# Attention of a tuned transformer kernel: maxima turned late, a longer lead of the query-major scores, rests in PSUM, value products in runs of two blocks

## The reference, cut to what matters

```python
# attention A: 16 query heads of 16, one shared key head and value head, causal
scores = einsum('bnhd,bmd->bhnm', q, k) / sqrt(16);  scores = where(causal, -inf, scores)
out = einsum('bhnm,bmd->bnhd', softmax(scores), v)
# attention B: 16 heads with their own keys and values, causal, with an ALiBi bias
scores = einsum('bhqd,bhkd->bhqk', q, k) / sqrt(16) + slope[h] * (kpos - qpos)
```

## Time and profile before

| | |
|---|---|
| median of the runs | 1035.86 us |
| profiled execution: its time, its span | 1033.63 us, 1031.9 us |
| TensorE busy (matmuls) | 964.2 us, 93% |
| VectorE busy | 760.6 us, 74% over the kernel |
| ScalarE, GpSimd busy | 570.4 us, 411.3 us |
| first attention, first piece to last value product | 55.0 to 296.7 us |
| second attention, the same | 571.9 to 806.5 us |
| a step inside an attention | 27.8 us |

### The profile page before, as it was taken

One profiled execution on the slowest core, in us unless ns is written; L12 is line 12 of the kernel. 1 busy time (PEld: TensorE's weight loads), 2 busy tenths in 40 slices (PEclk: granted clock), 3 DMA queues, 4 the chain that ended last, 5 costly groups with the idle time before them and its releaser, 6 DMA issues.

```text
span 1031.9 us, 19370 instructions
## 1 busy us (share of the span) xinstructions
PE 964.2 (93%) x6370; PEld 613.2 (59%) x6370; DVE 760.6 (74%) x2132; ACT 570.4 (55%) x1078; POOL 411.3 (40%) x434
## 2 busy tenths in 40 slices
PE   4888999999889999999998989999999899999998
PEld 3433333333358889988886433333334588899887
DVE  6798999999256776447778979999992568764475
ACT  4525777777744335653354647777777533466332
POOL 3420634333435417625843102323225361374570
PEclk9879999999989999999999989999999999999999
DMA  4721212210105215733249523334401251266351
GB/s 142 193 46 30 47 44 44 44 44 9 49 26 203 80 47 173 181 122 120 67 116 218 118 36 69 61 70 77 76 13 44 84 173 53 82 190 160 117 183 48
DMA packets 66755, 95.40 MB, mean 92 GB/s; under 512 B 19669, under 2 KB 50821, under 8 KB 64599
## 3 DMA queue, kind: packets, MB, share of 16 engines
q1 hardware_dynamic: 46645, 52.74, 19.0%
q10 hardware_dynamic: 13100, 22.53, 8.6%
q0 software_dynamic: 6912, 18.88, 7.0%
HBM read 66.79 MB, written 26.67 MB: 91 GB/s over the span
## 4 chain that ended last, share of the span: by engine, by line
PE 71%; DVE 16%; issue 4%; DMA 3%; ACT 3%; POOL 2%; SPq 1%; ACTq 0%; DVEq 0%; POOLq 0%
PE o_ps L1101 13%; PE st_ps L1084 8%; PE su_ps L1043 7%; PE st_ps L293 7%; PE st_ps L294 7%; PE st_ps L295 7%; PE o_ps L1241 4%; PE st_ps L1043 4%; PE su_ps L1241 3%; DVE mab L1729 3%; PE su_ps L1147 3%; DVE unread L1725 3%; PE st_ps L1276 2%; DVE xn L1604 1%; PE su_ps L293 1%
## 5 line engine op out<-in xcount | busy, mean ns | idle before, releaser
L1446 ACT ACTIVATE pt<-st_ps 128x512 f32<-128x512 f32 (+1 forms) x584 | 312.0, 596 | 161.3 <-PE st_ps L1084 153.5
L1084 PE MATMUL st_ps<-qs,ks 99*128 99x512 bf16 (+9 forms) x768 | 211.8, 328 | 4.3 <-DMA qs<-nmx 2.4
L807 POOL TENSOR_SCALAR_AFFINE_SELECT pt<-pt 128x512 f32<-128x512 f32 x120 | 74.7, 641 | 311.7 <-ACT pt L1446 311.7
L1043 PE MATMUL su_ps<-ks,qs 102*128 102x512 bf16 (+7 forms) x538 | 155.2, 330 | 11.5 <-DVE mc L1725 4.5
L1101 PE MATMUL o_ps<-pt,vp 128*32 128x512 f32 (+3 forms) x1536 | 156.6, 505 | 0.0
L1725 DVE CUSTOM_DVE_ANT_0 unread<-su_ps,cst 128x384 f32<-128x384 f32 (+3 forms) x324 | 143.0, 479 | 16.2 <-PE su_ps L1043 15.5
L1729 DVE TENSOR_REDUCE mab<-su_ps 128x1 f32<-128x512 f32 (+2 forms) x181 | 118.6, 683 | 7.2 <-PE su_ps L1043 5.1
L1043 PEld LDWEIGHTS su_ps<-ks,qs 96*128 96x128 bf16 (+1 forms) x538 | 48.5, 98 | 122.4 <-DVE mab L1729 44.4
L888 POOL DMA_INDIRECT rows_in<-rows,source x80 | 79.1, 989 | 97.5 <-DVE source L1988 73.7
L1084 PEld LDWEIGHTS st_ps<-qs,ks 99*128 99x128 bf16 (+2 forms) x768 | 73.1, 98 | 63.5 <-ACT pt L1446 16.6
L1472 ACT CAST hh<-hf 128x512 fp32r<-128x512 f32 x64 | 39.7, 620 | 123.2 <-DVE hf L1943 123.2
(11 more groups left out here) (234 smaller groups left out, 1975.7 us busy)
## 6 DMA issues: line engine op xcount, KB each, us to landing
wu_raw<-w_units_dram SPq DMA_DIRECT2D x32, 384.0 KB, 3.2
outs<-rows_out ACTq DMA_DIRECT2D x40, 256.0 KB
q_parts<-hml SPq DMA_DIRECT2D x16, 384.0 KB, 3.1
wexp_raw<-w_units_dram SPq DMA_DIRECT2D x16, 384.0 KB, 6.5
inv<-inverses SPq DMA_DIRECT2D x128, 32.0 KB, 1.8
rows<-xn SPq DMA_DIRECT2D x8, 512.0 KB, 6.2
qs<-q_parts ACTq DMA_DIRECT2D x10, 384.0 KB
k_parts<-hml SPq DMA_DIRECT2D x8, 384.0 KB, 2.9
```

The lines of the kernel that those rows point to most:

```text
L807: pool.affine_select(block, block, [[0, 4], [1, P]], ALU.is_ge, 0.0, base=0, channel_multiplier=-1).then_inc(masked, 1)
L1043: last = pe.matmul(out_b[:, c0:c0 + width], query_columns(s, slice(0, rows), j0 + a, P * qt, P * qt + P), key_stack(l, s)(j0 + a)[0:rows, ...
L1084: last = pe.matmul(out_b[:, at:at + hi - lo], key_stack(l, s)(j)[0:rows, P * kt:P * kt + P], query_columns(s, slice(0, rows), j, lo, hi), ...
L1446: act.activation(exponentials(S, q)[:, j, 0:width_of(s, q)], bank[KM_BANKS[i % len(KM_BANKS)]][:, 0:width_of(s, q)], ACT.Exp, scale=1 / np ...
```

## The change

1. The value products are issued in runs: `(0,), (1, 2), (3, 4), (5, 6), (7, 8)` of each later step, each behind the second piece of the block two after the last of the run. In step 0 they are `(0,)`, `(1, 2)`, `(3, 4)`, `(5, 6)` and `(7, 8, 9)`, the last one ahead of the first piece of step 1. The run `(7, 8)` of a step stands in the next step's block 1, as block 8 did.
2. `lead` is 0.36 where it was 0.2.
3. For steps 2 to 6 of each attention (`turned_late`) the transposition stands behind the third unit of the following step; unit numbers, and with them the banks, are counted accordingly. VectorE does the join at once and the negative parts three units later. SyncE sends these maxima ahead of `gather_sums(S, 0)`.
4. The rest of the maxima is written back to the PSUM bank of the transposition (`turned[:, P:2 * P]`) where it went to the SBUF tile `nmr`. The bank is given free by the last of the four operations, where the second gave it free.
5. The reciprocals stand ahead of units 10 and 26, where they stood ahead of 6 and 27.

```diff
+def value_runs():
+    first = len(FIRST_BLOCKS)
+    runs = {2: (0,), 6: (3, 4), 8: (5, 6)}
+    early = {HALF_BLOCKS: (1, 2), first: (7, 8, 9)}
+    for s in range(1, STEPS):
+        for run in ((0,), (1, 2), (3, 4), (5, 6), (7, 8)):
+            runs[block_base(s) + run[-1] + PV_LAG] = tuple(block_base(s) + q for q in run)
+    return runs, early, runs.pop(block_base(STEPS) + PV_LAG - 1)
+
+def turned_late(s):
+    return 2 <= s < STEPS - 1
+
+def unit_number(S, u):
+    s = S % STEPS
+    if u == NSU - 1 and turned_late(s):
+        return unit_base(S) + u + UNITS_AHEAD
+    if u < UNITS_AHEAD and turned_late(s - 1):
+        return unit_base(S) + u - 1
+    return unit_base(S) + u
+UNITS_AHEAD = 3
...
     for s in range(2, STEPS):
-        for u, t in enumerate(s - 1 - lead + through):
+        for u in range(NSU):
+            t = s - 1 - lead + (passed[u] if turned_late(s - 1) else through[u])
             while at[n] < t - 1e-9 or u > 1 and n < FIRST_PIECES - 1:
                 n += 1
-            behind[n].append((s, u))
+            if u < NSU - 1 or not turned_late(s):
+                behind[n].append((s, u))
+            if u == UNITS_AHEAD - 1 and turned_late(s - 1):
+                behind[n].append((s - 1, NSU - 1))
...
-UNITS_BEHIND = [units_behind_pieces(l, 0.2) for l in range(2)]
+UNITS_BEHIND = [units_behind_pieces(l, 0.36) for l in range(2)]
-INVERT_AT, DIVIDE_BEHIND = (6, 27), (2, 4)
+INVERT_AT, DIVIDE_BEHIND = (10, 26), (2, 4)
...
-                    if n in (HALF_PIECES, FIRST_PIECES):
-                        for early in range(i - PV_LAG, i):
-                            values(l, 0, early)
+                    if j == 0:
+                        for b in EARLY_RUNS.get(i, ()):
+                            values(l, *place_of_block(b))
                     key_major(l, s, q, j)
-                    if j == PV_BEHIND and i >= PV_LAG and i not in [...]:
-                        values(l, *place_of_block(i - PV_LAG))
+                    if j == PV_BEHIND:
+                        for b in RUNS.get(i, ()):
+                            values(l, *place_of_block(b))
...
-            def negative_parts(src, rows, a, taken, count, done):
+            def negative_parts(turned, rows, a, taken, count, done):
+                src, rest = turned[:, 0:P], turned[:, P:2 * P]
                 dve.tensor_scalar(nmx[rows, a, 0, :], src, -1.0, None, ALU.mult).then_inc(nm_step, 1)
-                dve.scalar_tensor_tensor(nmr[rows, :], src, -1.0, nmx[rows, a, 0, :], ALU.mult, ALU.subtract).then_inc(taken, 1)
+                dve.scalar_tensor_tensor(rest, src, -1.0, nmx[rows, a, 0, :], ALU.mult, ALU.subtract).then_inc(nm_step, 1)
-                dve.tensor_copy(nmx[rows, a, 1, :], nmr[rows, :]).then_inc(nm_step, 1)
+                dve.tensor_copy(nmx[rows, a, 1, :], rest).then_inc(nm_step, 1)
-                dve.tensor_tensor(nmx[rows, a, 2, :], nmr[rows, :], nmx[rows, a, 1, :], ALU.subtract).then_inc(nm_done, 1)
+                dve.tensor_tensor(nmx[rows, a, 2, :], rest, nmx[rows, a, 1, :], ALU.subtract).then_inc(taken, 1)
...
+                            if u == UNITS_AHEAD and turned_late(s):
+                                maxima_parts(l, s)
                             maximum(l, s + 1, u)
-                        maxima_parts(l, s + 1)
+                        join_maxima(l, s + 1)
+                        if not turned_late(s + 1):
+                            maxima_parts(l, s + 1)
```

More of the change, by code:

```diff
@@ L161, in place_of_block, with run_behind, taking @@
     return next((s, i - block_base(s)) for s in reversed(range(STEPS)) if i >= block_base(s))
+def value_runs():
[6 more added lines that the diff above has]
+    return runs, early, runs.pop(block_base(STEPS) + PV_LAG - 1)
+PV_LAG = 2
+RUNS, EARLY_RUNS, LAST_RUN = value_runs()
+def run_behind(b):
+    return next((i for i, run in RUNS.items() if b in run), None)
+def taking(b):
+    i = run_behind(b)
+    if i is None:
+        i = next((i for i, run in EARLY_RUNS.items() if b in run), None)
+    return None if i is None else 4 * i + 3
 def unit_base(S):
     return NSU * S - len(range(0, S, STEPS))
+def turned_late(s):
[8 more added lines that the diff above has]
+UNITS_AHEAD = 3
 ADDED = [[u for u in range(len(SU)) if SU[u][5] and not by_matmul(s, u)] for s in range(STEPS)]
@@ L186, in added_before @@
     at = added_turn(S, u) - 2
-    return unit_base(added_units(S)[at][0]) + added_units(S)[at][1] + 1 if at >= 0 else 0
+    return unit_number(*added_units(S)[at]) + 1 if at >= 0 else 0
 def units_behind_pieces(l, lead):
@@ L452, in program @@
         half_in, first_in, turned_half, half_taken = [sem("half_in0"), sem("half_in1")], sem("first_in"), sem("turned_half"), sem("half_taken")
[L453 removed]
+        su_ready, su_used, mc_done, nm_step = (sem(n) for n in ("su_ready", "su_used", "mc_done", "nm_step"))
         st_ready, p_ready, pv_done, ou_done, inv_done, ot_done = (
@@ L635, in send_half @@
             def send_half(l, half):
-                sp.wait_ge(nm_done, maxima_count(l, 0, half))
+                sp.wait_ge(half_taken, 2 * l + half + 1)
                 for part in range(3):
@@ L710, in attention @@
                         load_unit(l, 0)
-                    if s + 1 < STEPS:
+                    if s + 1 < STEPS and not turned_late(s + 1):
                         send_maxima(l, s + 1)
@@ L1132, in attention @@
                         output_projection(l, FC_BEHIND[4 * q + j])
-                for q in range(len(LATER_BLOCKS) - PV_LAG, len(LATER_BLOCKS)):
-                    values(l, STEPS - 1, q)
+                for b in LAST_RUN:
+                    values(l, *place_of_block(b))
             def output_projection(l, tt):
@@ L1449, in attention @@
                             load_stack(l, s + 2, LOAD_BEHIND.index(n))
-                        if s and n == 4 * PV_LAG - 1:
+                        own = piece_base(s) + n
+                        if s and own == taking(block_base(s - 1) + last_of(s - 1, 1)[0]):
                             take_output(S - 1, 1)
-                        if n == 4 * (last_of(s, 0)[0] + PV_LAG + 1) - 1:
+                        if own == taking(block_base(s) + last_of(s, 0)[0]):
                             take_output(S, 0)
```

35 lines of the change are left out of this document (19 added, 16 removed).

## The result

The changed kernel takes 1063.42 us (median of 4 runs, 1061.68 to 1068.51), the kernel before, beside it on the same chip, 1035.35 us: ratio 1.028, interval [1.024, 1.032]. It is slower, and 1059 was predicted. The profiled execution has a span of 1061.8 us.

What follows compares the result with a forecast made beforehand. TensorE and VectorE, both near their limit and tied by three banks, were taken as the bound. Terms 11.4 + 10.4 + 1.6 = +23.4 us on 1033.6 gave 1057.0, plus 2.2 for the median: 1059, range 1036 to 1067 (likeliest case 1053 to 1067).

Steps and rivals of the forecast that it cites:

- The rule for a stretch: Between value products: 2.09 us (2.95 with a run of two) plus VectorE's first N-3 units, or TensorE's time if that decides.
- VectorE's account: In a later step VectorE has 24.7 us of work and 4.5 dry, giving the same as the walked 29.2 us.
- the first rival: TensorE is the bound and the mergings count: 26 us faster, 1010 us; chance 0.11.
- At least 1.1 us dry per run of two: Behind each run of two VectorE idles at least 1.1 us; under 0.5 us would show the forecast wrong.
- Waits of TensorE's units for L1725 and L1729 of some 3 us per step: Sign in a later step: TensorE's units wait some 3 us in all for VectorE at these lines.
- Steps 0 and 1: Start of both attentions: longer lead and runs end step 0 5.6 us later, step 1 takes 0.4 less; +10.4 us.
- The second rival: Front-loaded units are paid back in full and the long run sees full clock: 1049 to 1053 us; chance 0.27.
- steps 6 and 7: End of both attentions: step 6 net +1.5 us, step 7 -0.7 us in each; +1.6 us for both.
- The fourth rival: TensorE's longer waits bring the clock down inside most steps, over +14 us: above 1067 us; chance 0.08.
- three mergings: In step 7, without units, output projections keep ScalarE ahead, so three mergings give their full 0.24 us each: -0.7 us.
- 1 to 2 us a step: Price if the reciprocal ahead of unit 10, some 5 us behind the copy of the sums, is uncovered.
- +0.3 a turned step from L1740: In 10 turned steps L1740, the last operation on the maxima, falls from 0.60 to 0.28 us, saving 0.3 us each.

Runs made afterwards that it cites:

- VectorE relieved: Changed kernel and kernel before, each with maxima over every other key only (half the maxima, output changes): ratios 0.980 and 0.973 to the kernel before.
- mended kernel: Changed kernel, runs of two kept, with lead growing over step 2's units, reciprocals ahead of units 12 and 33, step 7's transposition later: ratio 1.016 to before.
- the last turn later: Changed kernel with only step 7's transposition moved from behind piece (5,3) of step 6 to behind (7,0): ratio 1.021 to the kernel before.

## Why the prediction was right, and where it was off

The rule for a stretch held. The five stretches of a later step were walked at 2.85, 7.2, 6.6, 5.8 and 6.8; the trace has 2.85, 7.12, 6.60, 6.04 and 6.71, 29.32 us for 29.2. VectorE's account was 24.7 of work and 4.5 dry; it is 24.62 and 4.55. A run takes the 1.86 of the sum. The mechanism is shown from two sides: the runs alone make a step 29.85, and with VectorE relieved the changed kernel's step, runs and all, is a little shorter than that of the kernel before. That refutes the first rival, TensorE as the bound, for full maxima; its gain begins to show only where VectorE has time to spare.

Three details were off. "At least 1.1 us dry per run of two": the dry times are 0.51 to 1.60, and 0.51 is only just above the 0.5 that was to count as a sign against the forecast. The four together, 4.27, are near the 4.4 of the prediction, so the sum over the step hides the spread; that it comes from the small units (128 and 256 columns), which leave VectorE more or less work in its banks, is my reading and not tested. "Waits of TensorE's units for L1725 and L1729 of some 3 us per step": the timeline has three such waits in the step, 0.88 us in all. A matmul's modelled length of 0.39, where the next can begin after 0.22, covers a part of each wait; against the step with VectorE relieved (25.95) the loss is 3.4. And VectorE's work "falls from 25.0 to 24.7": the earlier trace rows have 25.36, so it fell by 0.74 and not by 0.3, and the match of 24.7 with 24.62 is in part luck. The kernel with the runs alone, whose last operation takes 0.60 as before, has 24.99 of work; what makes up the difference is open.

Steps 0 and 1 were +10.4 and are +10.6, and the parts hold as well: step 0 ends 5.1 and 5.3 us later (5.6 was taken), step 1 takes 0.3 less and 0.5 more (0.4 less was said). In front of the long run stand the 15 units behind piece 39. The clock is 0.50 from 98.31 to 108.55, so the run of three blocks has its first 2.0 us at half clock and takes 3.25, between the 2.3 and the 4.4 worked out for the two clocks (4.43 in the second attention of the mended kernel, where all of it is at 0.50). The second rival, that the long run sees the full clock and the units' time comes back, is refuted. One part was in no sum: the first value run of the second attention is at half clock too (593.83, 1.87 us for 1.00). TensorE's timeline at the end of step 0, against the earlier trace rows:

```profile
106.57 3.31 PE L1155 MATMUL o_ps<-pt,vp 128*32 128x384 f32 x32
109.81 0.39 PE L1138 MATMUL st_ps<-qs,ks 99*128 99x512 bf16 x1
```

The mis-sized term is steps 6 and 7: "Both attentions: +1.6", measured +7.4. The wait for the join was foreseen (some 1.8, it is 1.65), and the DMA wait ahead of step 7 is gone as foreseen but for 0.19 in the second attention. What was not: the clock fell to 0.50 at 279.2 (and at 798.0), and the run there took 3.18 us instead of 1.86. The stretch is 7.25 us where the second attention has 5.71 at full clock, and there it is 9.04 for 7.54 one stretch earlier; the fall costs 1.5 us in each attention, 3.0 of the 5.8 us that the term was short. The fourth rival, that the clock comes down inside the steps too, so came true once per attention and not in most steps. Without the fall step 6 would still be 2.0 and 2.4 us longer instead of the 1.5, which leaves 1.4 unexplained. TensorE's timeline:

```profile
273.34 0.28 PE L1122 MATMUL su_ps<-cst,mc 128*32 128x128 f32 x1 [1.65 <-DVE mc L1813]
273.99 1.93 PE L1155 MATMUL o_ps<-pt,vp 128*32 128x512 f32 x24
276.94 0.88 PE L1138 MATMUL st_ps<-qs,ks 99*128 99x512 bf16 x2 [0.26 <-ACT pt L1500]
278.40 1.59 PE L1138 MATMUL st_ps<-qs,ks 99*128 99x512 bf16 x3 [0.59 <-ACT pt L1500]
279.92 3.25 PE L1155 MATMUL o_ps<-pt,vp 128*32 128x512 f32 x24
```

And step 7, where three mergings were to give 0.7 in each attention, gave nothing, the last 1.4. From the first single run of the step to its end it takes 21.56 us in both kernels. The windows, changed kernel and then before, show TensorE busy 0.42 less, and one wait for ScalarE of 0.42 in its place:

```profile
290.71:312.27 21.56, 21.14 (x160) 11.01 (x156) 8.59 (x29) 14.64 (x29) 11.90 (x15) 1.00 0.10 27
```
```profile
275.12:296.68 21.56, 21.56 (x160) 10.64 (x156) 7.82 (x26) 14.92 (x29) 12.04 (x16) 1.00 0.10 27
```
```profile
306.23 0.39 PE L1138 MATMUL st_ps<-qs,ks 99*128 99x512 bf16 x1 [0.42 <-ACT pt L1500]
```

My sentence that the output projections "keep ScalarE ahead there" was wrong. The wait fits a longer run that delays the pieces that feed ScalarE, as it delays the units that feed VectorE; no run here tests that alone.

The steps 2 to 5 of the second attention held a second, smaller surprise: +7.49 for +5.7. A price of "1 to 2 us a step" was named for the reciprocal ahead of unit 10, if its cover went; the wait came ahead of unit 26, 0.13, 0.45 and 0.45 us in the steps that took 29.56, 29.88 and 29.88 us (and 0.67 in step 1). With the lead alone it was 21.9 us of the second attention.

The total of 1059 came out closer than its parts. The attentions were forecast 23.4 us longer and are 31.6; the 1.1 us ahead of them and the 2.8 less between and behind them were in no term, and the runs' median is 28.1 above that of before where the spans differ by 29.9. The step's rule is right by its mechanism; that the total is off by 4.4 us and not by more is in part luck.

About the forecast's +0.3 a turned step from L1740: the four operations take 1.2 us as I took them, but in the kernel with the rests in PSUM alone the gain is nil, as it fell into a product's pause. In the changed kernel they stand three units behind the join, away from that place; how much of the 0.3 to 0.4 us that is left for the late turn is their shortness and how much the covered wait was not separated.

What stays open: why the clock falls in step 6. In the second attention of the changed kernel it fell at 798.04, within the wait for the join (796.59 to 798.24) and ahead of that step's waits for ScalarE:

```profile
798.24 0.40 PE L1122 MATMUL st_ps<-cst,mc 128*32 128x128 f32 x1 [1.65 <-DVE mc L1813]
```

The mended kernel with runs of two has no wait for the join, and the clock fell all the same in both attentions (a run of 3.26 us at 275.77, behind a wait for ScalarE of 0.59). The kernel with the last turn later has no wait for the join either and the same wait of 0.59, and its clock fell in the second attention but not in the first; with half the maxima there is a wait for the join (0.73) and that of 0.59, and it did not fall. So neither wait by itself decides it.

## What to carry to other kernels

Merging work that blocks an engine saves its own overhead (a run of two takes 1.86 us here for 2.00 of two single ones) and lengthens the pause that everybody behind it sees; compare the pause with what the buffers between the engines hold (here three banks are 1.83 us of VectorE, against the 2.95 by the rule until it has the next unit), and merge only where the fed engine has time to spare. A reciprocal or any wait for a transfer that is tied to a counter of work moves when the work is moved: shift its place with the lead. A term taken "for nothing" because another engine hides it should be walked on that engine too, ScalarE as well as VectorE (the 0.7 of step 7 here, of which nothing came).

## What the runs showed of the hardware that I had not expected

- The same code between the attentions takes 283.4 us on one chip (296.68 to 580.05) and 301.1 on another (297.53 to 598.58), at a clock of 0.99 and 0.98 with TensorE busy 269 and 274 us of the window, while a step inside the attention is 27.79 us on both. Absolute times of different chips are not to be compared there.
- VectorE reads every other element of PSUM at no extra price: a reduce over 256 of 512 columns at a stride of two took 0.42 us, as long as another operation of VectorE over 256 adjacent ones, where the reduce over 512 takes 0.68.
- With the lead alone, waits of 1.5 to 2.0 us for a 16-column reciprocal's input went with 3.0 to 4.6 us in the steps 2 to 5 of the second attention (30.8 to 32.4 for 27.8). TensorE's wait behind each was followed by matmuls at half clock (0.61 on average over the 3.4 us from 722.20).
